# Adaptive-norm attention block in float32: the opening up to the first score rebuilt, part of it moved beside the first scores

## The reference

```python
mod = (silu(c) @ wmod).reshape(6, 512)          # sa, ca, ga, sb, cb, gb
ga, gb = sign(.) * maximum(abs(.), 0.25)        # for ga and gb
h = layernorm(x) * (1 + ca) + sa
x = x + ga * attention(h)                       # 32 heads, causal, 1024 positions
h = layernorm(x) * (1 + cb) + sb
x = x + gb * down(silu(gate(h)) * up(h))        # int8-valued weights, inner size 1376
```

## Time and profile before

| | us |
|---|---|
| median of 3 runs (851.72 to 857.37) | 854.62 |
| the profiled execution's own time | 855.57 |
| its span, first to last instruction | 853.8 |
| first score (PE L610) starts at | 135.57 |
| first score of window 1, of window 2 | 196.15, 257.22 |

### The profile page before, as it was taken

The page is one execution under the profiler, slowest core; times in us unless marked ns, Lnnn a source line. Parts: engine busy times, 40 slices in busy tenths (PEclk is TensorE's granted clock), DMA queues, the critical chain, the costliest instruction groups (busy, mean ns, idle before and its releaser), DMA issues.

```text
span 853.8 us, 10443 instructions
## 1 busy us (share of the span) xinstructions
PE 793.7 (93%) x3968; PEld 530.2 (62%) x3968; DVE 551.0 (65%) x836; ACT 272.2 (32%) x402; POOL 146.5 (17%) x113
## 2 busy tenths in 40 slices
PE   5678897999999999999999999999898899999997
PEld 5667544555555555555555555544587788886886
DVE  3355694896896997988978978867565333222342
ACT  2361003333333333343333333343344232222120
POOL 1320031221221321411302401010134000000111
PEclk9886697999999999999999999999899899999999
DMA  8300724023213303321330335046000032220000
GB/s 345 116 0 1 211 52 111 20 56 89 51 25 89 75 21 69 74 52 38 74 85 5 74 83 214 2 159 212 1 1 0 10 102 74 74 65 1 25 37 38
DMA packets 35904, 60.46 MB, mean 71 GB/s; under 512 B 4144, under 2 KB 16176, under 8 KB 34064
## 3 DMA queue, kind: packets, MB, share of 16 engines
q1 hardware_dynamic: 34656, 57.11, 23.7%
q10 hardware_dynamic: 1200, 2.69, 0.9%
HBM read 32.40 MB, written 2.10 MB: 40 GB/s over the span
## 4 chain that ended last, share of the span: by engine, by line
PE 64%; DVE 20%; issue 9%; POOL 2%; ACT 2%; DMA 2%; SPq 1%; POOLq 0%; DVEq 0%; ACTq 0%
PE PS L710 14%; PE PS L610 6%; PE PS L554 6%; PE PS L625 6%; DVE PR L1184 6%; PE PS L680 5%; PE PS L611 5%; PE PS L612 5%; DVE NMa L1096 4%; DVE NMb L1096 3%; PE PS L544 2%; PE PS L482 2%; PE PS L570 2%; PE PS L513 2%; PE PS L614 2%
## 5 line engine op out<-in xcount | busy, mean ns | idle before, releaser
L836 ACT ACTIVATE PR<-PS 128x1024 f32<-128x1024 f32 (+1 forms) x144 | 133.0, 929 | 255.2 <-PE PS L612 240.4
L1096 DVE TENSOR_REDUCE NMa<-PS 128x1 f32<-128x512 f32 (+3 forms) x216 | 138.7, 662 | 50.0 <-PE PS L558 42.7
L554 PE MATMUL PS<-KH,Q 96*128 96x512 f32 (+3 forms) x384 | 135.5, 414 | 3.9 <-DVE TQ L1081 1.4
L610 PE MATMUL PS<-Q,KH 97*128 97x512 f32 x288 | 131.7, 457 | 2.6 <-DMA Q<-NM 2.6
L710 PE MATMUL PS<-Q 128*128 128x512 f32 (+1 forms) x528 | 123.2, 396 | 5.1 <-DVE Q L1258 4.5
L710 PEld LDWEIGHTS PS<-Q 128*128 128x128 f32 (+1 forms) x528 | 99.2, 188 | 28.2 <-DVE Q L1258 4.7
L1184 DVE TENSOR_TENSOR PR<-PR 128x2048 f32<-128x2048 f32 (+3 forms) x56 | 109.3, 1951 | 10.2 <-ACT PR L836 8.9
L611 PE MATMUL PS<-Q,KL 96*128 96x512 f32 x288 | 114.7, 398 | 0.0
L612 PE MATMUL PS<-Q,KH 96*128 96x512 f32 x288 | 113.9, 396 | 0.0
L554 PEld LDWEIGHTS PS<-KH,Q 96*128 96x128 f32 x384 | 69.8, 197 | 62.3 <-issue 38.0
L610 PEld LDWEIGHTS PS<-Q,KH 97*128 97x128 f32 x288 | 56.0, 195 | 35.3 <-issue 17.1
(11 more groups left out here) (157 smaller groups left out, 1002.1 us busy)
## 6 DMA issues: line engine op xcount, KB each, us to landing
Q<-TQ SPq DMA_DIRECT2D x64, 384.0 KB, 5.3
PR<-in_wmod SPq DMA_DIRECT2D x6, 1024.0 KB, 7.0
RT<-in_wo SPq DMA_DIRECT2D x4, 1024.0 KB, 5.1
TQ<-in_wo SPq DMA_DIRECT2D x4, 1024.0 KB, 4.9
WI<-in_gate_w SPq DMA_DIRECT2D x10, 256.0 KB, 3.1
WI<-in_up_w SPq DMA_DIRECT2D x10, 256.0 KB, 3.3
DI<-in_down_w SPq DMA_DIRECT2D x10, 256.0 KB, 3.6
TQ<-in_x ACTq DMA_DIRECT2D x2, 1024.0 KB, 10.3
```

Of the source, the lines that this page charges most:

```text
L554: ins = pe.matmul(bank[:, i * w:(i + 1) * w], M.Q[0:KR, g % 2, 0, qt // 4, h0 + i, qs], M.KH[0:KR, lo:lo + w], start=(i == 0), stop=(i == ...
L610: pe.matmul(dst, M.KH[0:KR + 1, ks], M.Q[0:KR + 1, w % 2, 0, qb, :, qs], start=True, stop=False)
L836: act.activation(tiles, banks, ACT.Exp).then_inc(S_.p, 1)
L1096: dve.tensor_reduce(dst, PS[:, bank_of(turn), 0:n * w].rearrange("p (h k) -> p h k", k=w), axis=AX.X, op=ALU.max, negate=True).then_inc(S_ ...
```

## The change

- x is loaded tile by tile by SP, right behind the first two `wmod` blocks and the input weights. The ACT queue loads nothing at the start.
- Scale and shift move into the input weights: ACT makes `WAH` with the scale (4 instructions of 288), DVE the rest `WAL` (4 of 288), and PE multiplies the shift with the input weights (`shift_projected`, one column a matmul), added in each projection by two matmuls with a row of ones. `modulate` goes. ACT rounds the turned tile from PSUM (512 wide), DVE takes the rest from PSUM; the normalisation of the tile, the copy of V and the rotary sum of the key go from DVE to POOL.
- The first group's weights are folded after tile 3, its queries of half 0 made after tile 6, those of half 1 after the last tile; then only the 11 maxima parts of half 0, which get a transposition and a transfer of their own. The first score waits for these alone.
- Group 0's other 27 parts and all queries of group 1 stand beside the first 10 units of window 0, at a cost of 0 in the table; the first score of half 1 waits for the second transfer, which SP issues after the four of group 1's half 0. The rest of window 0 has the maxima of group 1 (until place 0.93 instead of 0.78), the queries of group 2, both gates and one column product; window 1 has the other.
- Queries of groups 1 and 2 (`HANDED`): ACT copies `even` and `odd` to SBUF, POOL makes the four products and the two sums. For all groups ACT, not DVE, makes the high part of `lat`.
- The three late `wmod` blocks are issued on the ACT queue after the last tile, the fourth by SP in window 0.

```diff
+HANDED = (1, 2)
...
-def maxima_places():
+def maxima_places(begin, end):
...
+def opening_places():
+    opened = NUNIT_FIRST / NUNIT
+    parts = range(FIRST, len(PARTS))
+    places = [(opened * 0.9 * (k - FIRST) / len(parts), ("part", 0, k), 0.0) for k in parts]
+    places += group_places(1, [(opened * 1.45 * place, name, 0.0) for place, name, _ in QUERY_PLACES])
+    return places + [(opened * 0.92, ("join", 0), 0.0), (opened * 0.98, ("rows", 0, 1), 0.0)]
...
+    elif w == 0:
+        places += opening_places()
+        places += group_places(1, maxima_places(0.29, 0.93))
+        places += group_places(2, [(0.25 + 0.7 * place, name, busy) for place, name, busy in QUERY_PLACES])
+        places += group_places(0, [(0.50, ("modrow", 0), 0.7), (0.62, ("modrow", 1), 0.7), (0.75, ("mod", 2), 0.2)])
...
+FIRST_QUERIES = [[(kind, 0, hf) for kind in ("even", "odd", "lat", "split")] for hf in range(2)]
+FIRST_MAXIMA = [("part", 0, k) for k in range(FIRST)] + [("rows", 0, 0)]
...
     send_queries(0, 0)
     send_queries(0, 1)
-    load_weights(1)
-    load_mod(5)
+    send_first_maxima(0)
     send_queries(1, 0)
-    send_maxima(0)
+    send_first_maxima(1)
...
@@ pe_program @@
+    turn_inputs(0)
+    shift_projected()
+    turn_inputs(1)
+    for st in range(NS + 2):
         if st < NS:
+            project_inputs(st)
+        if st + 2 < NS:
+            turn_inputs(st + 2)
+        if st == 3:
+            for key in FIRST_FOLDS:
+                side(key)
+        if 0 <= st - 2 < NS:
+            turn_latents(st - 2)
+        if st == NS - 2:
+            for key in FIRST_QUERIES[0]:
+                side(key)
...
@@ act_program @@
+    def queries_copied(kind, g, hf):
+        turn = TURN[(kind, g, hf)]
+        act.wait_ge(S_.side, turn + 1)
+        act.wait_ge(S_.re, 2 * (2 * g + hf))
+        act.activation(M.RT[:, ("even", "odd").index(kind), :], PS[:, bank_of(turn), :], ACT.Copy).then_inc(
+            S_.free[turn % 3], 1)
...
+    for key in FIRST_QUERIES[1]:
+        side(key)
+
+    act.wait_ge(S_.ql, NS)
+    for n in (4, 5, 2):
+        act.dma_start(M.wmod[n], t["wmod"][MOD_ORDER[n]]).then_inc(S_.wm[n], 16)
...
@@ dve_program @@
+    mod_first(0)
+    mod_first(1)
+    moments(0)
+    inverse_root(0)
+    moments(1)
+    weights_rest()
+    inverse_root(1)
+    h_low(0)
+    shift_split()
...
+    for st in range(NS + 2):
+        if st + 2 < NS:
+            inverse_root(st + 2)
+        if st + 1 < NS:
+            h_low(st + 1)
+        if st + 3 < NS:
+            moments(st + 3)
+        if st < NS:
+            scale(st)
+        if 0 <= st - 2 < NS:
+            latents_low(st - 2)
...
@@ pool_program @@
+    def normalise_input(st):
+        pool.wait_ge(S_.rs, st + 1)
+        if st >= 2:
+            pool.wait_ge(S_.tr, st - 1)
+        pool.tensor_scalar(M.xn[:, st % 2, :], M.x[:, st, :], M.mv[:, st, 0:1], M.rstd[:, st:st + 1],
+                           ALU.subtract, ALU.mult).then_inc(S_.xn, 1)
...
+    def rotate_even(g, hf):
+        cols = slice(hf * 512, hf * 512 + 512)
+        half = 2 * (g - 1) + hf
+        pool.wait_ge(S_.free[TURN[("even", g, hf)] % 3], freed(("even", g, hf)))
+        pool.tensor_tensor(M.RT[:, 3, :], M.RT[:, 0, :], M.sin[:, cols], ALU.mult).then_inc(S_.rp, 1)
+        pool.wait_ge(S_.rp, 4 * half + 1)
+        pool.tensor_tensor(M.RT[:, 0, :], M.RT[:, 0, :], M.cos[:, cols], ALU.mult).then_inc(S_.rp, 1)
```

More of the change, by code:

```diff
@@ L51 @@
 PARTS = maxima_parts()
+FIRST = sum(part[0] < NS // 2 for part in PARTS)
+HANDED = (1, 2)
 def softmax_scale():
@@ L80 @@
 NUNIT = len(UNITS)
+NUNIT_FIRST = sum(STEPS[s][0] == 0 for s, i in UNITS)
 VALUE_LAG, ADD_LAG = 3, 2
@@ L559, in maxima_part, with maxima_rows @@
         ins.then_inc(S_.side, 1)
-    def maxima_rows(g):
-        bank = side_bank(TURN[("rows", g)])
-        pe.wait_ge(S_.nm, g + 1)
-        pe.transpose(bank[0:HG * NS, 0:P], M.NMa[:].rearrange("p f h n -> p (f h n)"), M.ident[:]).then_inc(S_.side, 1)
+    def maxima_rows(g, hf):
+        bank = side_bank(TURN[("rows", g, hf)])
+        if hf == 0:
+            for k in range(FIRST - 3, FIRST):
+                pe.wait_ge(S_.free[TURN[("part", g, k)] % 3], freed(("part", g, k)))
+        else:
+            pe.wait_ge(S_.nm, g + 1)
+        shown = M.NMa[:, 0:hf + 1].rearrange("p f h n -> p (f h n)")
+        pe.transpose(bank[0:(hf + 1) * HG * NS // 2, 0:P], shown, M.ident[:]).then_inc(S_.side, 1)
     def denominator(w, qb):
@@ L815, in side @@
             weights_high(key[1])
+        elif key[0] in ("even", "odd") and key[1] in HANDED:
+            queries_copied(key[0], key[1], key[2])
+        elif key[0] == "lat":
+            latent_high(key[1], key[2])
         elif key[0] == "split":
@@ new lines, in mod_first, with weights_rest @@
+    def mod_first(n):
+        dve.wait_ge(S_.m, n + 1)
+        dve.tensor_scalar(M.mod_col[:, n, :], PS[:, 6 + n, 0:KD], 1.0 if n == 0 else 0.0, None, ALU.add).then_inc(S_.mc, 1)
+    def weights_rest():
+        dve.wait_ge(S_.wah, 1)
+        for k in range(KD):
+            ins = dve.scalar_tensor_tensor(out=M.WAL[:, k, :], in0=M.WA[:, k, :], scalar=M.mod_col[:, 0, k:k + 1],
+                                           in1=M.WAH[:, k, :].bitcast(F32), op0=ALU.mult, op1=ALU.subtract)
+        ins.then_inc(S_.wal, 1)
@@ L1372, in side @@
             weights_low(g)
+        elif kind == "even" and g in HANDED:
+            rotate_even(g, key[2])
+        elif kind == "odd" and g in HANDED:
+            rotate_odd(g, key[2])
         elif kind == "odd" and g > 0:
@@ L1378, in side @@
             normalise(g, key[2])
-    for _, name, _ in QUERY_PLACES:
-        side((name[0], 0) + name[1:])
-    for name in PROLOGUE:
-        if name[-1] == "next":
-            side((name[0], 1, name[1]))
+    normalise_input(0)
+    normalise_input(1)
+    for st in range(NS + 2):
+        if st + 2 < NS:
+            normalise_input(st + 2)
+        if st < NS:
+            keys(st)
+        if st == 3:
+            for key in FIRST_FOLDS:
+                side(key)
+    pool.wait_ge(S_.tables, 32)
     for w in range(G):
```

468 lines of the change are left out of this document (237 added, 231 removed).

## The result

The changed kernel takes 889.57 us in the median of four runs (886.11 to 898.57), the kernel before on the same chip 854.22: a ratio of 1.0428, 95% interval 1.0342 to 1.0514. The forecast was 843 with a range of 831 to 857. It is slower by 4%, where faster was expected, and by a way that no rival described at its full size.

The account below looks back on a forecast made before the run. It took PE to bound the windows, and a chain across engines the opening. Opening -48.1, window 0 +33.6, window 1 +3.3, latent part -1.0 give -12.2 on the profiled 855.57: 843.4, stated as 843, range 831 to 857.

Parts of the forecast that it names:

- B, window 0: Window 0, from 60.6 to 94.2 us: +33.6, ends +25 and +43.
- Behind two standstills the clock comes back late: 1.5 each: Window 0: slow clock behind two standstills, priced by the first units at 136 us; 3.0 us in the sum.
- The forecast's own sign of being wrong: Window 0: a length over 102 us would show the prediction wrong; 94 was forecast.
- C: Later windows: +3.3 us in window 1 for a column product, -1.0 over five windows for the latent part on ACT.
- The rest of B: Window 0 without the clock's 3.0: first ten units 31.3 us, remaining units 55.7, exposed join and transfer at the end 4.2.
- POOL's chain or SP's queue: Window 0, first ten units: rotary products on POOL, or the second maxima transfer behind queued sends, both give 31.3 us.
- A, the opening: Up to the first score, at 87.5 us instead of 135.57: -48.1; ends 82.9 and 95.5.
- The forecast's round of a tile: Opening: rounding, root, reciprocal, POOL's normalisation at 1.3, turn and four handovers take 3.7 us a tile.
- Rival 2: Window 0: group 2's POOL products cause two standstills, 3 us each plus 1.5 of clock; +9, 852.5 us; chance 0.23.
- Rival 3: Opening: each projection waits for the whole tile round, 8.1 us a tile; +31, 874 us; chance 0.12.

Follow-up runs that it names:

- Experiments 1 and 12: 1: changed kernel with waits for maxima filled with mask products, 877.33 us; 12: best kernel without its 24 mask products, 857.36 us.
- experiment 2: Changed kernel with the rotary products of head groups 1 and 2 on VectorE again instead of GpSimd: 883.91 us.
- experiment 3: Changed kernel with half 1's maxima sent by SyncE ahead of that half's queries for the upper keys: 893.75 us, single run.
- best kernel: Changed kernel with normalising, rotary products and latent high part (from group 4) on VectorE; gates, column products and 24 mask products in waits: 845.52 us.
- Experiment 6: Changed kernel with the input tiles normalised on VectorE instead of GpSimd: 878.26 us.
- Experiment 5: Changed kernel with the latent high part copied by VectorE again in every group, at the old planned cost: 890.55 us.
- experiment 8: Changed kernel with the second half's maxima and second group's queries worked out ahead of the first score again: 883.31 us.

## Why the prediction was wrong

The forecast was -12.2 on the profiled execution, the result +30.5; 42.7 us are to be found.

**B, window 0: the step that failed is the clock** ("Behind two standstills the clock comes back late: 1.5 each"). It was priced by the first units at 136 us of the earlier trace rows; the clock was back there 4.3 us behind the first score, and the earlier trace rows already has 2.2 us for it (0.88 over 18.30). In the changed kernel the clock is at 0.50 for 12.8 us behind the first standstill and for 19.3 behind the second. In slices of 1 us PE loses 22.9 us in window 0, where 3.0 were forecast: 16.2 behind these two standstills, and 6.7 behind the wait at 170.7 and from 191.2 on, for which the forecast had no term. Experiments 1 and 12 show that the waits do it. The forecast's own sign of being wrong, a window 0 over 102 us, came with 117. C had no clock term at all: 7.5 in window 1, of which 2.4 are at its start and 5.1 behind the column product.

**The rest of B came out right in its number, and only in part by its reasons.** Without its clock loss of 6.6 (slices of 1 us; the table's mean gives 7.1) the first ten units are 31.2, forecast 31.3. That is luck. The forecast had POOL's chain or SP's queue end them; experiment 2 took POOL's products away and they did not get shorter, and the queue was empty (experiment 3). What they consist of is PE's work, 24.3 us net of the clock (forecast 25.1), and 5.9 of waiting for the joined maxima and their transfer, a chain that the forecast priced for the end of the window and not here. POOL's products took the 1.28 of the earlier trace rows, but for one of 2.66 beside a sum of DVE, and ACT idled twice for POOL's sums, 9.1 us in all, without holding up PE.

From unit 10 on it is 79.3 - 16.3 = 63.0 against 59.9. PE's busy time in it is 55.7 net of the clock, as forecast, although a gate took 3.04 us at full clock (eight instructions in a row, the first at 159.94, the next work behind them at 162.98) where 2.0 was taken from a pair alone between other products in the earlier trace rows, and a column product 3.73 (best kernel), forecast 3.3; so other work was priced too high by as much. The chain of join, transposition and transfer was exposed at the end, as forecast (waits of 1.65 and 2.59). The 3.1 on top are two waits for maxima that DVE had not taken yet, 1.82 and 1.30.

**A, the opening: 8.9 us late, one term mis-sized above the others.** POOL's normalisation was taken as 1.3 from two-input rows of the same width; it is 2.07. The forecast's round of a tile becomes 4.5 with it, and 4.4 was measured: the projections start from 28.66 to 63.37, 34.7 us for seven tiles, 4.2 of it the folds and queries that the forecast counted there. So the sum of the round held, and this term gives 0.8 ahead of the first projection and 4.6 over the seven tiles. Two others were too low: the shift product took 3.02, forecast 1.5, and from the last projection to half 1's queries complete 18.8 us passed, forecast 16.4. The transfer took 6.2 us and not 2, near the forecast's 6.8. Experiment 6 moved the first score 9.8 earlier with the instruction at 0.55 on VectorE, to 86.64, forecast 87.5. That it lands so near is luck: its tiles go round in 3.1 us, less than the 3.7 forecast with 1.3 for the instruction, and this pays for the two low terms. The Trainium skill's GPSIMD Engine Reference (section 3.1), weighed in the forecast with 0.77 us for a one-input loop of 512, is further off still; for this form, with two values per partition, the measurement decides.

**C, later windows.** -0.2 a window was taken for the latent part on ScalarE, within ends of -4 and +2 for five; it is +0.65 in each of windows 2 to 5, so 3.5 us worse together and outside those ends if window 1 is like them. Experiment 5 takes it away again.

These are 8.9 + 19.9 + 3.0 (the remainder of window 0) + 7.5 + 0.6 (the remainder of window 1) + 3.5 - 0.7 (what follows window 5) = 42.7.

**The rivals.** Rival 2 had the right place, window 0, and a mechanism that fits what experiment 2 took away (up to 5 us), but the clock in it at 1.5. Rival 3's ring did not close: 4.4 us a tile, not 8.1. The case that came, slower by way of window 0, had no chance in the forecast, because each rival took over the same 1.5. The clock's term had no upper end. The earlier trace rows showed 0.52 from 86 to 96, with PE busy all the time, and the same trace has PE waiting 3.18 us up to 101.99 and the clock at half until 109 behind it: 3 to 5 us for each standstill, twice or three times what was taken.

## What to carry to other kernels

Moving work off the front of a kernel makes new waits at the seams, and TensorE can pay for a wait twice: the wait itself, and then a time at half clock, here from 3 us (behind 1.82 at 170.7) to 19 (behind unit 10's wait), and 26 in experiment 8. Look for a standstill behind which the profile's clock stays down, and fill it, with real work if some is ready, else with products that nobody reads: here 24 of them were worth 10 to 12 us. And price an instruction by its own form: the same normalisation is 0.55 us on VectorE and 2.07 on GpSimd.

## What the runs showed of the hardware

- The clock's fall and return are not alike. A standstill of 2.30 us behind a run of one-column products was enough to halve it; in the changed kernel 19.3 us of PE busy without a gap (134.21 to 153.5) passed before it came back. The Trainium skill's TensorE: Matmul & The Clock Gate (section "HAM oscillation — how this bites in real kernels") says that waits for transfers send the array back to its slow clock, again at each wait, and advises an order that keeps it busy. These traces agree as to the fall; the long way back was the surprise.
- In window 1 a run of 32 one-column products, busy in the trace, goes with a fall of the clock without any standstill ahead of it (0.83 from 224.55 to 225.55, then 0.50 to 235), as in this chain of PE's instructions of the changed kernel (start, us). The opening's 64 ran at 1.00, so the run alone does not make the fall:

```profile
222.06 4.14 PE L513 MATMUL PS<-silu_c,wide 128*128 128x1 f32 x32
226.12 1.06 PE L578 MATMUL PS<-WK,WN 64*128 64x32 f32 x4
227.11 0.79 PE L664 MATMUL PS<-Q,KH 97*128 97x512 f32 x1
227.70 0.63 PE L665 MATMUL PS<-Q,KL 96*128 96x512 f32 x1
```

  The score product behind it takes 0.63 us instead of the 0.39 of full clock. In the best kernel, twelve wide products stood behind the run at 119.40, and the clock stayed at 1.00; behind the other one, at 174.76, it was 0.53 through the run and its twelve, and back at 1.00 with the first score of window 1. What tells the two apart was not found.
